# Shorter prefix sums for the first batch and a new order of its steps, in a transformer layer with an FFT attention on one Trainium2 core

## The reference

```python
q  = (x @ W_q.T).reshape(B, S, 16, 32)
kv = (x @ W_kv.T).reshape(B, S, 16, 32)
qf, kvf = l2_normalize(fft(q)), l2_normalize(fft(kv))
kvf = cumsum(kvf, axis=1)                  # over the 512 rows of a batch
values = ifft(qf * kvf).real.reshape(B, S, D)
x = x + values @ W_o.T
...
gate = silu((x @ fp8(gate_w)) * gate_scale)
up   = (x @ fp8(up_w)) * up_scale
x = x + ((gate * up) @ fp8(down_w)) * down_scale
```

## Time and profile before

| | before |
|---|---|
| median of 3 runs | 418.65 us (418.07 to 419.58) |
| the profiled execution | 418.57 us |
| its span, first to last instruction | 416.8 us |
| TensorE busy | 408.6 us, 98% |
| VectorE busy | 298.1 us, 72% |
| ScalarE busy | 193.4 us, 46% |
| GpSimd busy | 109.2 us, 26% |
| granted clock of TensorE, mean | 0.999 |
| DMA | 33.55 MB, mean 81 GB/s |

### The profile page before, as it was taken

How to read it: one execution, slowest core, us unless ns; L and a number is a source line. 1 busy time by engine, 2 the same in 40 slices (tenths; PEclk the granted TensorE clock), 3 DMA queues, 4 the chain that set the end, 5 groups by cost and what they waited for, 6 DMA issues and landing times.

```text
span 416.8 us, 5552 instructions
## 1 busy us (share of the span) xinstructions
PE 408.6 (98%) x1921; PEld 205.8 (49%) x1921; DVE 298.1 (72%) x516; ACT 193.4 (46%) x324; POOL 109.2 (26%) x114
## 2 busy tenths in 40 slices
PE   8999999999999999999999999999999999999995
PEld 4744454445555554454555555454444444445442
DVE  5998998999989699997984972167855853422235
ACT  3687656586736245445242563345533341132220
POOL 0133641015254137043541013032462001300003
PEclk9999999999999999999999999999999999999999
DMA  8997547600281153232112015401112041200002
GB/s 260 269 253 240 167 113 165 165 0 2 42 238 51 26 77 70 58 125 77 28 26 50 2 25 102 76 36 66 26 26 52 0 76 26 101 2 0 2 0 101
DMA packets 57691, 33.55 MB, mean 81 GB/s; under 512 B 49472, under 2 KB 50112, under 8 KB 57536
## 3 DMA queue, kind: packets, MB, share of 16 engines
q1 hardware_dynamic: 57232, 32.93, 31.0%
q10 hardware_dynamic: 432, 0.28, 0.2%
HBM read 17.44 MB, written 4.19 MB: 52 GB/s over the span
## 4 chain that ended last, share of the span: by engine, by line
PE 86%; DVE 4%; POOL 2%; DMA 2%; ACT 2%; issue 1%; SPq 1%; POOLq 0%; ACTq 0%; DVEq 0%
PE bu L477 19%; PE bg L477 18%; PE bd L504 17%; PE ba L376 14%; PE ba L422 8%; PE bd L376 3%; PE bd L344 2%; DMA h<-x_dram 1%; PE bd L422 1%; PE ba L395 1%; DMA qk<-qk 1%; PE bd L362 1%; PE bu L422 1%; POOL h L1674 1%; DVE y L1143 1%
## 5 line engine op out<-in xcount | busy, mean ns | idle before, releaser
L477 PE MATMUL bu<-hT,gu 128*128 128x512 f16 x384 | 90.7, 379 | 0.0
L477 PE MATMUL bg<-hT,gu 128*128 128x512 f16 x376 | 89.0, 379 | 0.3 <-ACT sl L757 0.3
L1258 DVE SCALAR_TENSOR_TENSOR ff<-bu,us,sl 128x512 f32<-128x512 f32 x47 | 35.2, 748 | 53.9 <-PE bu L477 50.5
L757 ACT ACTIVATE sl<-bg,gs 128x512 f32<-128x512 f32 x48 | 32.9, 686 | 78.1 <-PE bg L477 77.0
L376 PE MATMUL ba<-wf,xT 128*128 128x512 f16 x288 | 63.2, 379 | 0.0
L477 PEld LDWEIGHTS bu<-hT,gu 128*128 128x128 f16 x384 | 37.5, 98 | 45.5 <-DVE ff L1258 0.6
L477 PEld LDWEIGHTS bg<-hT,gu 128*128 128x128 f16 x376 | 35.6, 98 | 43.6 <-issue 4.1
L504 PE MATMUL bd<-dw,fu 128*128 128x512 f32 x192 | 51.1, 411 | 0.1
L1674 POOL TENSOR_TENSOR h<-ff,h 128x512 f32<-128x512 f32 x14 | 17.5, 1269 | 121.3 <-DVE ff L1300 121.3
L376 PEld LDWEIGHTS ba<-wf,xT 128*128 128x128 f16 x288 | 27.9, 98 | 34.1 <-issue 1.1
L1643 POOL TENSOR_TENSOR xs<-xn,xs 128x512 f16<-128x512 f32 x15 | 20.4, 1368 | 78.5 <-ACT xs L669 78.5
(11 more groups left out here) (210 smaller groups left out, 540.7 us busy)
## 6 DMA issues: line engine op xcount, KB each, us to landing
h<-x_dram SPq DMA_DIRECT2D x16, 256.0 KB, 4.1
out_dram<-h SPq DMA_DIRECT2D x14, 256.0 KB, 2.0
hT<-w_q_dram SPq DMA_DIRECT2D x4, 256.0 KB, 4.0
gu<-w_kv_dram SPq DMA_DIRECT2D x4, 256.0 KB, 4.1
hT<-gate_w_dram SPq DMA_DIRECT2D x2, 512.0 KB, 3.7
hT<-up_w_dram SPq DMA_DIRECT2D x2, 512.0 KB, 6.0
gu<-woT_dram SPq DMA_DIRECT2D x1, 1024.0 KB, 5.2
hT<-down_w_dram SPq DMA_DIRECT2D x2, 512.0 KB, 5.0
```

The lines of the kernel that those rows point to most:

```text
L477: m = e.matmul(bk[:, :], gu[:, c, 4 * w + k, col:col + P], hT[:, b % 2, part, k, :], start=k == 0 and part == 0, stop=k == KT - 1 and part ...
L757: e.activation(sl[:, n % 2, :], bg[:, :], ACT.Silu, scale=gs[:, i:i + 1]).then_inc(a_silu, 1)
L1258: e.scalar_tensor_tensor(out=ff[:, n % 2, :], in0=bu[:, :], scalar=(us if b < HALF else us2)[:, i:i + 1], in1=sl[:, n % 2, :], op0=ALU.mul ...
```

## The change

It has two parts. First, for batch 0, GpSimd adds the scaled k of tiles 0 and 1 (`pool_sum`), ScalarE and GpSimd split this sum into a high and a low part (`act_sum`, `pool_sum_low`), and the prefix sums of tiles 2 and 3 meet it in place of both tiles. They take 4 and 6 matmuls in place of 6 and 8. The parts lie where the transposed product of tile 3 comes later. Second, steps of batch 0 and of the first slices stand in another order on all five engines. Within `pe_o`, the three products are ordered by part, and each part is waited for separately.

```diff
-    order += [("pT", 0, 0), ("tri", 0, 2), ("tri", 0, 3), ("pT", 0, 1), ("o", 0, 0), ("pT", 0, 2), ("o", 0, 1),
-              ("pT", 0, 3), ("o", 0, 2), ("o", 0, 3), ("qk", 1, 0, 0), ("qk", 1, 0, 1)]
+    order += [("pT", 0, 0), ("tri", 0, 2), ("o", 0, 0), ("pT", 0, 1), ("tri", 0, 3), ("pT", 0, 2), ("o", 0, 1),
+              ("pT", 0, 3), ("qk", 1, 0, 0), ("o", 0, 2), ("o", 0, 3), ("qk", 1, 0, 1)]
...
+        sum_parts = zT[:, 3, :, :]
...
         def pe_tri(e, b, t):
             i = AT["tri", b, t]
-            tiles = range(t + 1) if b == 0 else (t,)
+            whole = [] if b > 0 or t == 0 else [ks[:, :, 0, :]] if t == 1 else [sum_parts] + [ks[:, :, s, :] for s in range(2, t)]
...
+            for n, parts in enumerate(whole):
                 for part in range(2):
+                    if n == 0 and t == 2:
+                        e.wait_ge(p_sumlo if part else a_sum, 1)
+                    e.matmul(ba[i][:, :], tr16[:, 1, :], parts[:, part, :], start=n == 0 and part == 0, stop=False)
+            for part in range(2):
+                e.wait_ge(p_ks if part else a_ks, 4 * b + t + 1)
+                c = e.matmul(ba[i][:, :], tr16[:, 0, :], ks[:, part, t, :],
+                             start=not whole and part == 0, stop=part == 1)
...
         def pe_o(e, b, t):
-            if b == 0:
-                e.wait_ge(a_pT, t + 1)
-                e.wait_ge(v_pT, t + 1)
-            else:
+            if b > 0:
                 e.wait_ge(d_zT[t], 32 * b)
-            if b == 0 and t == 0:
-                e.wait_ge(a_wolo, KT)
-            for j in range(KT):
-                for part_p, part_w in ((0, 0), (0, 1), (1, 0)):
+            for part_p, part_w in ((0, 0), (1, 0), (0, 1)):
+                if b == 0 and part_w == 0:
+                    e.wait_ge(v_pT if part_p else a_pT, t + 1)
+                for j in range(KT):
+                    if b == 0 and t == 0 and part_w == 1:
+                        e.wait_ge(a_wolo, j + 1)
...
+        def act_sum(e):
+            e.wait_ge(p_sum, 1)
+            e.activation(sum_parts[:, 0, :], sums[:, :], ACT.Copy).then_inc(a_sum, 1)
...
+        def pool_sum(e):
+            e.wait_ge(v_kn, 2)
+            e.tensor_tensor(sums[:, :], qk[:, 0, 1, :], qk[:, 1, 1, :], ALU.add).then_inc(p_sum, 1)
+
+        def pool_sum_low(e):
+            e.wait_ge(a_sum, 1)
+            e.tensor_tensor(sum_parts[:, 1, :], sums[:, :], sum_parts[:, 0, :], ALU.subtract).then_inc(p_sumlo, 1)
...
             pe_tri(e, 0, 2)
+            pe_o(e, 0, 0)
+            pe_pT(e, 0, 1)
             pe_tri(e, 0, 3)
-            pe_pT(e, 0, 1)
-            pe_o(e, 0, 0)
             pe_o(e, 0, 1)
...
             act_ks(e, 0, 1)
+            act_sum(e)
...
+            act_pT(e, 0)
             act_wo_low(e, 0)
-            act_pT(e, 0)
...
-            act_ks(e, 1, 1)
             act_fu(e, 2)
             act_silu(e, 3)
+            act_ks(e, 1, 1)
...
-            act_root0(e, 2, range(NT))
             act_row(e, 1, 1)
...
-            act_xh(e, 2, 0)
             act_silu(e, 7)
...
             act_silu(e, 9)
+            act_root0(e, 2, range(NT))
             act_ks(e, 1, 3)
...
             act_silu(e, 10)
+            act_xh(e, 2, 0)
             act_zh(e, 1, 3)
...
             pool_ks(e, 0, 0)
+            pool_sum(e)
             pool_product(e, 0, 0)
             pool_ks(e, 0, 1)
+            pool_sum_low(e)
             pool_ks(e, 0, 2)
+            pool_product(e, 0, 1)
             pool_ks(e, 0, 3)
-            pool_product(e, 0, 1)
...
-            pool_xl(e, 2, 0)
             pool_product(e, 1, 1)
             pool_product(e, 1, 2)
             pool_ks(e, 1, 3)
             pool_product(e, 1, 3)
+            pool_xl(e, 2, 0)
```

More of the change, by code:

```diff
@@ L113, in build @@
         tu = sb("tu", [P, 2, 512], F32)
-        pT = sb("pT", [P, 2, 512], F32R)
+        sums = sb("sums", [P, 512], F32)
         h = sb("h", [P, 3, NT, 512], F32)
@@ L197, in build @@
         a_zh, v_zl = sem("act_zh"), sem("dve_zl")
+        p_sum, a_sum, p_sumlo = sem("pool_sum"), sem("act_sum"), sem("pool_sumlo")
         v_most, s_bound, a_bound, v_unit2, v_gus, p_dw = (
@@ L390, in pe_tri @@
                 e.wait_ge(a_tr, 1)
-            for s in tiles:
+            for n, parts in enumerate(whole):
                 for part in range(2):
[L393 to L396, removed]
+                    if n == 0 and t == 2:
[5 more added lines that the diff above has]
+                             start=not whole and part == 0, stop=part == 1)
             c.then_inc(s_tri, 1)
@@ L412, in pe_o @@
             vacant(e, ("o", b, t))
-            if b == 0:
-                e.wait_ge(a_pT, t + 1)
-                e.wait_ge(v_pT, t + 1)
-            else:
+            if b > 0:
                 e.wait_ge(d_zT[t], 32 * b)
-            if b == 0 and t == 0:
-                e.wait_ge(a_wolo, KT)
-            for j in range(KT):
-                for part_p, part_w in ((0, 0), (0, 1), (1, 0)):
+            for part_p, part_w in ((0, 0), (1, 0), (0, 1)):
[4 more added lines that the diff above has]
+                        e.wait_ge(a_wolo, j + 1)
                     m = e.matmul(ba[i][:, :], src[:, part_p, P * j:P * j + P], wo[:, part_w, j, :],
-                                 start=j == 0 and part_p == part_w, stop=j == KT - 1 and part_p == 1)
+                                 start=j == 0 and part_p == part_w, stop=j == KT - 1 and part_w == 1)
             m.then_inc(s_o, 1)
@@ L728, in act_row @@
             e.dma_start(qk[0:1, t, 1, :], qk[127:128, t, 1, :]).then_inc(d_carry, 16)
+        def act_sum(e):
+            e.wait_ge(p_sum, 1)
+            e.activation(sum_parts[:, 0, :], sums[:, :], ACT.Copy).then_inc(a_sum, 1)
         def act_pT(e, t):
             e.wait_ge(s_pT, t + 1)
+            if t == 3:
+                e.wait_ge(s_tri, 4)
             e.activation(pT_at(0, t)[:, 0, :], ba[AT["pT", 0, t]][:, :], ACT.Copy).then_inc(a_pT, 1)
@@ L885, in scalar_program @@
             act_hT(e, 0, 1)
+            act_sqrt2(e, 0, [2, 3])
             act_qk(e, 1, 1, 0)
-            act_sqrt2(e, 0, [2, 3])
             act_hT(e, 0, 2)
             act_qk(e, 1, 1, 1)
+            act_hT(e, 0, 3)
             act_qk(e, 1, 2, 0)
-            act_hT(e, 0, 3)
             act_qk(e, 1, 2, 1)
@@ L1399, in vector_program @@
             dve_o(e, 0, 2)
+            dve_o(e, 0, 3)
+            dve_ln2_head(e, 0, [2, 3])
+            dve_hT(e, 0, 0)
             dve_sum(e, 1, 0, 0)
-            dve_hT(e, 0, 0)
-            dve_o(e, 0, 3)
+            dve_ln2_tail(e, 0, [2, 3])
             dve_hT(e, 0, 1)
-            dve_ln2_head(e, 0, [2, 3])
-            dve_ln2_tail(e, 0, [2, 3])
             dve_hn(e, 0, 2)
@@ L1421, in vector_program @@
             dve_round(e, 6)
-            dve_stats1(e, 2, 2)
             dve_f(e, 0)
@@ L1452, in vector_program @@
             dve_fu(e, 4)
-            dve_xn(e, 2, 1)
+            dve_stats1(e, 2, 0)
             dve_round(e, 12)
@@ L1458, in vector_program @@
             dve_round(e, 13)
+            dve_stats1(e, 2, 1)
             dve_f(e, 7)
@@ L1467, in vector_program @@
             dve_o(e, 1, 0)
+            dve_stats1(e, 2, 2)
+            dve_stats1(e, 2, 3)
             dve_fu(e, 8)
+            dve_root0_head(e, 2, range(NT))
             dve_f(e, 9)
@@ L1473, in vector_program @@
             dve_zl(e, 1, 2)
+            dve_root0_tail(e, 2, range(NT))
+            dve_xn(e, 2, 0)
+            dve_xn(e, 2, 1)
             dve_f(e, 10)
@@ L1864, in sync_program @@
             sp_hT(e, 0, 3)
+            sp_weights(e, 7)
+            sp_weights(e, 8)
+            sp_x(e, 2, 3)
             sp_weights(e, 12)
@@ L1874, in sync_program @@
             sp_zT(e, 1, 2)
+            sp_xT(e, 2, 0)
             sp_zT(e, 1, 3)
```

12 lines of the change are left out of this document (1 added, 11 removed).

## The result

| | before | with the change |
|---|---|---|
| median of 6 runs | 418.75 us (418.07 to 419.58) | 421.43 us (421.16 to 421.76) |
| ratio, 95% interval | | 1.0064 (1.0052 to 1.0076) |
| the profiled execution, its span | 418.57, 416.8 us | 421.48, 419.7 us |

The kernel is 2.7 us slower. That is past the 1.26 us (0.3%) that the prediction calls the bound of no change, and past the 420.0 us at the high end of its range.

A forecast was written before the change was run, and what follows sets the result against it. TensorE, busy 408.6 of 416.8 us, was taken as the bound. Batch 0 and the silu gain 0.95 and 0.47 us, the later price is 1.67: +0.25 us on 418.57 gives 418.8 us, range 417.3 to 420.0.

The forecast's parts named there:

- I cost both at nothing: Batch 0: two added GpSimd instructions, 1.14 us each, fall into GpSimd's idle 3.02 and 2.89 us, costing nothing.
- 121 to 150 us: Stretch where batch 2's moved statistics delay VectorE and the SP queue; zl(1,2) forecast to end at 140.5 us.
- The moved split of tile 3: Batch 0: split now behind tile 1's product, ending near 49.3, wanted by tri(0,3) at 49.8; cost nothing.
- still makes its input at the same time: Batch 0: VectorE supplies GpSimd's product of tile 2 as before, so pT(0,2) starts at 53.14 instead of 54.09.
- 0.95, not 1.75: Batch 0's gain at pT(0,2): 0.95 us, not the 0.86 of removed matmuls plus the 0.89 wait.
- The silu at the gate of i = 4, 0.47 us: Near 99.56 us: ScalarE's silu goes ahead of the split of ks(1,1), ending TensorE's wait; gain 0.47 us.
- The price between the gate of i = 7 and o(1,3), 1.67 us: VectorE's added statistics and xT(2,0) ahead on the SP queue delay zT(1,3), so o(1,3); cost 1.67 us.
- the disturbance that I halved to 0.30: 121 to 150 us: VectorE's 0.60 us delay beside GpSimd's split may stay or vanish; half, 0.30, taken off.
- the first batch does not win: Rival: late GpSimd sums or product keep pT(0,2) at 54.09, the lost 0.95 us showing at o(1,3); 419.8 us, chance 0.06.
- The 1.42 us turn into a wait: In front of o(1,3): TensorE's 1.42 us gain becomes a DMA wait of 1.4 to 1.7 us, about 0.25 us lost.
- The rival against me: Silu's wait not won, both VectorE disturbances stay, o(1,3) 1.55 us late; 420.1 us, slower, chance 0.09.

The follow-up runs named there:

- e1: Changed kernel with its new order but batch 0's prefix sums as before, without the added GpSimd additions and ScalarE copy; 419.77 us, ratio 1.0033.
- e11: Changed kernel with only GpSimd's split of tile 3 moved back ahead of the product of tile 1; 420.64 us, ratio 1.0052.
- e4: Changed kernel with only GpSimd's order edited, same work, so its instructions keep out of VectorE's way; 419.55 us, ratio 1.0021.
- e6: Changed kernel with e4's GpSimd order and batch 2's first norm back at its early places; 417.85 us, ratio 0.9989.
- e8: e6 without the sum of two tiles: 14 prefix-sum matmuls, no added GpSimd or ScalarE instruction; 418.31 us, ratio 0.9991.
- e7: Kernel before with ScalarE's split of ks(1,1) moved behind the product's split of slice 2 and silu of slice 3; 418.45 us, ratio 0.9995.
- e2 again: Kernel before with only the sum of two tiles added, in the old order, repeated for its profile; 420.24 us in one run.
- e3: Changed kernel with the transposes of xT(2,0) issued behind those of zT(1,3) instead of ahead; 420.29 us, ratio 1.0038.
- e5: Changed kernel with the edits of e4 and e3 together; 418.89 us, ratio 0.9999.

## Why the prediction was wrong

- **The added GpSimd instructions, "I cost both at nothing": this step failed.** They fell into GpSimd's idle time as forecast, but the cost is not GpSimd's. They held up VectorE by 1.04 and 0.89 us. A part of the first fell into a gap of 0.68 us that VectorE had before; behind the second come the products of tiles 1 and 2, where the prediction itself says that VectorE has no gaps. Measured, 1.7 us (e1 against the changed kernel, part of it in the next point), where the sum has nothing. I had priced them by what cover TensorE would lose, and not asked who else the instruction stops. The same two rows that I used for 121 to 150 us, already showed it: two VectorE instructions that began while GpSimd ran ended 0.54 and 0.56 us after it.
- **The moved split of tile 3, also "nothing": failed the same way.** It was in time for its matmul (though the 0.5 us that the prediction leaves it don't come out of its own durations, by which the two nearly coincide), and lay across xn(1,0), 0.82 us longer; 0.85 us in e11. It was not in the sum.
- **The pace of VectorE in batch 0, "still makes its input at the same time": failed** as a result. pT(0,2) came 1.12 us later than before, not 0.95 earlier. These 2.07 us are most of the 2.6 between forecast and measurement. With the three meetings mended (e4) it comes 0.64 earlier; e6 and e8 reach 0.87 and 0.88. So the limit was near the forecast, and it is GpSimd's product of tile 2, as the working had it. That is why the shorter prefix sums are worth nothing up to qk(1,1,0) (e8), which the prediction's sum (0.95, not 1.75) already half said.
- **The silu at the gate of i = 4, 0.47 us: right**, 0.49 in the changed kernel and 0.42 in e7.
- **The price between the gate of i = 7 and o(1,3), 1.67 us: the right mechanism, 2.21 us.** The wait for the DMA is where it was forecast and 1.28 us long, xT(2,0) stands in front, and small waits came in front of o(1,1) and the gate of i = 10. The mis-sized term is the disturbance that I halved to 0.30: with the split of ks(1,3) moved back, the rounding's second instruction met it and took 2.06 us instead of 1.22. From the rounding of piece 13 to the end of zl(1,2) VectorE took 20.13 us, where 19.73 was forecast.

```profile
136.57 0.69 DVE L1077 TENSOR_SCALAR near<-own 128x1024 fp8e4<-128x1024 f32 x1
137.29 2.06 DVE L1080 SCALAR_TENSOR_TENSOR gu<-half,near 128x1024 f16<-128x1024 fp8e4 x1
```

```profile
136.88 1.39 POOL L1669 TENSOR_TENSOR ks<-qk,ks 128x512 f16<-128x512 f32 x1 [2.54 <-ACT ks L726]
```

- **The rival "the first batch does not win"** had the right consequence: what TensorE does not gain before the gate of i = 7 comes out in full at o(1,3). Its chance of 0.06 was too low, and it stopped at a gain of zero, where the loss was 1.13.
- **"The 1.42 us turn into a wait" was put wrongly.** The wait in front of o(1,3) is 1.28 us in the changed kernel, in e1 and in e4 alike, though TensorE reaches the gate of i = 7 at 75.21, 73.50 and 73.45. An earlier TensorE does not lengthen it, because VectorE's stretch moves with it; the price is that of the norm's new place and the queue's new order.
- **The rival against me**, VectorE's delay in full at 420.1 us, assumed that the silu's wait would not be won. It was; the slower side came about by the other term.

The Trainium skill (SBUF - State Buffer, section "SBUF: two separate sides") says that a VectorE instruction with two SBUF inputs, or in a fast mode with two ports, and a GpSimd instruction exclude each other for a whole instruction. The traces agree for five pairs shown here, by 0.8 to 1.1 us each: the three of the changed kernel's first batch, the third root step of e2 again and the rounding at 137.29. In two of them, inv's scaling and xn(1,0), VectorE reads one tensor, so they would have to be in the fast mode; no run shows the mode. For two inputs the Trainium skill limits this to a GpSimd instruction that reads SBUF, as all of these do. I had used that rule to make my sum smaller in one place and not looked for it in the place where instructions were added.

## What to carry to other kernels

Idle time of GpSimd is not free time: before work goes there, list VectorE's instructions under it, and move either until only kinds that were not held up lie beside it. Here those were reductions, statistics and products with an input from PSUM; scalings of one SBUF tensor and operations on two were held up. A small VectorE instruction paid as much here as a large one, about the rest of GpSimd's. And where a kernel is timed by one engine, a step taken out of it is worth only what the next releaser allows; here a queue of DMA transposes with 0.13 us of slack turned a late split and a transpose put ahead into waits.

## What was not expected of the hardware

The smallest instructions suffered most in proportion: the root's step on 64 columns took 1.12 us (changed kernel) or 1.07 (e2 again) instead of 0.22, as long as GpSimd's instruction had to run. GpSimd is held up too: in the kernel before, its first step of the product of tile 2, which began at 50.73 us, 0.07 us after a scaling of VectorE, took 1.20 us, and the same step of tiles 0 and 1 took 0.73.

Profiled executions of kernels with the same list of TensorE up to pT(0,0) reached it anywhere from 43.43 us (e4) to 44.61 us (e3). A difference of some tenths between kernels was readable only from a common matmul, and then down to some 0.24 us, while the medians of up to eleven runs left e5, e6, e7 and e8 undecided.
